# Cross attention's inverse sums: from a TensorE turn to a round trip through DRAM

## The reference, cut to what matters

```python
x = x + attn(layernorm(x), ...)
x = x + xattn(layernorm(x), ctx, ctx, mask, ...)     # the change is here
x = x + ffn(layernorm(x), ...)

# xattn, per sample b and head h (hc = 32, s = 512)
scores  = q @ k.T / sqrt(hc) + relative_term          # (s, s)
weights = softmax(scores, axis=-1)
context = weights @ v + relative_weights @ emb_v      # (s, hc)
out     = wo @ context                                # (256, s)
```

## Time and profile before

| what | us |
|---|---|
| median of 3 runs | 2598.54 |
| the profiled execution | 2598.18 |
| span of its instructions | 2596.4 |
| PE busy | 2411.5 |
| DVE busy | 2037.2 |
| ACT busy | 1128.8 |
| POOL busy | 1080.3 |
| distance of successive `near_back` (726.05 to 975.35, three rounds) | 83.1 |

### The profile page before, as it was taken

How to read it: one execution, slowest core, us unless ns; L and a number is a source line. 1 busy time by engine, 2 the same in 40 slices (tenths; PEclk the granted TensorE clock), 3 DMA queues, 4 the chain that set the end, 5 groups by cost and what they waited for, 6 DMA issues and landing times. The chain is left out here.

```text
span 2596.4 us, 40787 instructions
## 1 busy us (share of the span) xinstructions
PE 2411.5 (93%) x12856; PEld 1333.4 (51%) x12856; DVE 2037.2 (78%) x5965; ACT 1128.8 (43%) x2617; POOL 1080.3 (42%) x1564
## 2 busy tenths in 40 slices
PE   6889999999999999999988799999999999999985
PEld 4456655656566656665645344444444444444432
DVE  0466766777676776777664489999999999999997
ACT  1256666666666666666666221222222222222221
POOL 1133333333333333333332345555555555555552
PEclk9999999999999999999989899999999999999998
DMA  3034545444544545454446599999999999999996
GB/s 110 15 115 128 163 145 143 128 144 143 150 135 134 160 134 151 119 145 148 148 139 198 208 370 379 383 382 384 384 387 389 390 385 381 385 383 383 385 375 260
DMA packets 292741, 622.47 MB, mean 240 GB/s; under 512 B 162352, under 2 KB 163376, under 8 KB 292528
## 3 DMA queue, kind: packets, MB, share of 16 engines
q0 software_dynamic: 83968, 438.34, 44.4%
q1 hardware_dynamic: 174768, 80.85, 11.6%
q10 hardware_dynamic: 33792, 100.67, 11.3%
HBM read 577.80 MB, written 142.61 MB: 277 GB/s over the span
## 5 line engine op out<-in xcount | busy, mean ns | idle before, releaser
L1186 DVE CUSTOM_DVE_ANT_0 scores<-s_bank,added 128x512 f32<-128x512 f32 x512 | 350.2, 687 | 230.3 <-PE s_bank L661 185.4
L1501 PE MATMUL l_bank<-fold,xn_tf 128*128 128x512 f32 x992 | 435.5, 592 | 0.0
L996 ACT ACTIVATE probs<-scores,nmx 128x512 f32<-128x512 f32 x512 | 373.2, 729 | 129.4 <-DVE nmx L1186 125.4
L1479 POOL DMA_INDIRECT out_rows<-rows_out,rows_now x256 | 271.4, 1060 | 355.3 <-PE out_ps L1547 286.7
L1002 ACT COPY prob_t<-t_bank 128x512 f32<-128x512 f32 x512 | 299.3, 585 | 226.6 <-PE t_bank L671 226.1
L593 POOL TENSOR_TENSOR added<-mask_add,band 128x136 f32<-128x136 f32 (+1 forms) x512 | 247.6, 485 | 337.4 <-DVE nmx L1186 336.5
L1470 POOL DMA_INDIRECT in_rows<-rows_in,rows_now x256 | 310.3, 1212 | 134.3 <-DVE hid L1740 66.8
L639 PE MATMUL a_bank<-fold 128*128 128x256 f32 (+1 forms) x1024 | 305.2, 442 | 20.7 <-ACT fold L917 7.0
L671 PEld LDWEIGHTS t_bank<-ident,probs 128*128 128x128 f32 x2048 | 235.9, 141 | 165.5 <-issue 107.7
L671 PE MATMUL t_bank<-ident,probs 128*128 128x128 f32 x2048 | 313.4, 279 | 5.3 <-ACT prob_t L1002 3.2
L1593 ACT COPY sims<-l_bank 128x512 f32<-128x512 f32 x124 | 72.7, 586 | 555.5 <-PE l_bank L1501 555.5
(11 more groups left out here) (193 smaller groups left out, 3509.9 us busy)
## 6 DMA issues: line engine op xcount, KB each, us to landing
rows_in<-in_in_b_dram ACTq DMA_DIRECT2D x16, 2048.0 KB, 8.7
rows_out<-in_out_a_dram ACTq DMA_DIRECT2D x16, 2048.0 KB, 9.0
rows_in<-in_in_a_dram ACTq DMA_DIRECT2D x16, 1024.0 KB, 8.1
rows_out<-in_out_b_dram ACTq DMA_DIRECT2D x16, 1024.0 KB, 5.2
rel_scratch<-rel_pad SPq DMA_DIRECT2D x16, 640.0 KB, 3.0
band<-rel_scratch SPq DMA_DIRECT2D x512, 20.0 KB, 2.3
prob_scratch<-probs SPq DMA_DIRECT2D x512, 20.0 KB, 2.6
near<-prob_scratch SPq DMA_DIRECT2D x64, 156.1 KB, 3.1
```

Of the source, the lines that this page charges most:

```text
L996: nc.scalar.activation(prob_tile(s % PSLOTS), scores[:, s % 2, :], ACT.Exp, bias=nmx[:, s:s + 1], scale=-1.0, accum_out=lsum[:, s:s + 1]). ...
L1186: nc.vector.tensor_tensor_reduce(out=scores[:, s % 2, :], in0=s_bank[s % HPT][:, 0:L], in1=added[:, s % 2, :], scale=-1.0, scalar=-NEG, op ...
L1479: nc.gpsimd.indirect_dma_start(out_rows[:, h, :], None, rows_out, bass.IndirectOffsetOnAxis(rows_now[:, odd, h:h + 1], 0)).then_inc(out_lo ...
L1501: ins = nc.tensor.matmul(l_bank[c % 2][:], xn_t[:, k, :], fold[:, k, c * BANK:(c + 1) * BANK], start=(k == 0), stop=(k == KD - 1))
```

## The change

The widening copy (L1198), the wait before it, the turn on PE (L677) and the copy on ACT (L1007) are gone, with the step `SPREAD_LAG`. SP gets two new steps in each group. `store_sums` waits for `linv_ready`, now raised by the reciprocal, and writes the 128x4 inverse sums to DRAM turned, as 512 single elements. `spread_sums` waits until they have landed, and reads each of the four rows back to 32 partitions of `linv_t`, which now has two halves. `evict` waits for these four loads. `weigh` now waits only for `acc` to be emptied. Both steps stand after `store_windows` in SP's group; `near_back` moves between the two of group 7. The store of x3 and all that follows in the queue come behind them.

```diff
--- before.py
+++ after.py
@@ -139,7 +139,7 @@
         PACK, PB, OUT, X2, STATS3, POWER3, X3 = 4, 5, (6, 8), (7, 9), (10, 11), 12, 16
         LOAD_FOLD, FOLD, STORE_FOLD = 8, 29, 4
         EARLY_TURN, EARLY_SIMS, EARLY_SEARCH, EARLY_PICK = 11, (14, 18, 22, 26), (2, 2, 3, 3), 6
-    TURN_LAG, SUM_LAG, SPREAD_LAG, WEIGH_LAG, EVICT_LAG = 3, 5, 6, 8, 9
+    TURN_LAG, SUM_LAG, WEIGH_LAG, EVICT_LAG = 3, 5, 8, 9
     TOP_STEPS = 2 * TOPK // 8
     FOLD_VALUES_AT = 16
     SCORE_LATE = (16, 20)
@@ -223,6 +223,7 @@
         return FOLD_JOBS.index((kind, n))
 
     rel_scratch = nc.dram_tensor("rel_scratch", [(P + 1) * ROW], F32, kind="Internal").ap()
+    linv_dram = nc.dram_tensor("linv_dram", [2, HPT, P], F32, kind="Internal").ap()
     prob_scratch = nc.dram_tensor("prob_scratch", [(P + 1) * ROW], F32, kind="Internal").ap()
 
     with ExitStack() as ctx:
@@ -299,8 +300,7 @@
         nmx = sb("nmx", [P, STEPS])
         lsum = sb("lsum", [P, STEPS])
         linv = sb("linv", [P, STEPS])
-        linv_wide = sb("linv_wide", [P, HPT, HC])
-        linv_t = sb("linv_t", [P, P])
+        linv_t = sb("linv_t", [P, 2, P])
         probs = sb("probs", [P, PSLOTS * PROW])
         prob_t = sb("prob_t", [P, 2, HPT, QT_N, P])
         raw_q, raw_k = (prob_t[:, i].rearrange("p g k q -> p (g k q)").rearrange("p (k d) -> p k d", d=D)
@@ -356,8 +356,8 @@
         added_ready = sem("added_ready")
         exp_done = sem("exp_done")
         linv_ready = sem("linv_ready")
-        linv_turned = sem("linv_turned")
-        linv_kept = sem("linv_kept")
+        linv_stored = sem("linv_stored")
+        linv_loaded = [sem(f"linv_loaded{i}") for i in range(2)]
         near_written = [sem(f"near_written{i}") for i in range(2)]
         near_loaded = sem("near_loaded")
         near_packed = sem("near_packed")
@@ -448,6 +448,22 @@
                     n = ROW - QUAD + 1
                     sp.dma_start(near[g * QUAD:(g + 1) * QUAD, :, :].rearrange("r s w -> r (s w)")[:, 0:n],
                                  src[:, 0:n]).then_inc(near_loaded, 16)
+
+            def store_sums(r, n):
+
+                wait(sp, linv_loaded[n % 2], (r * (GROUPS // 2) + n // 2) * 16 * HPT)
+                sp.wait_ge(linv_ready, r * GROUPS + n + 1)
+                with nc.allow_non_contiguous_dma(reason="512 single elements"):
+                    sp.dma_start(linv_dram[n % 2].rearrange("h q -> q h"),
+                                 linv[:, n * HPT:(n + 1) * HPT]).then_inc(linv_stored, 16)
+
+            def spread_sums(r, n):
+
+                sp.wait_ge(linv_stored, 16 * (r * GROUPS + n + 1))
+                wait(sp, acc_emptied, r * GROUPS + n - 1)
+                for g in range(HPT):
+                    sp.dma_start(linv_t[g * HC:(g + 1) * HC, n % 2, :],
+                                 linv_dram[n % 2, g].partition_broadcast(HC)).then_inc(linv_loaded[n % 2], 16)
 
             def write_relative(b):
 
@@ -494,10 +510,12 @@
                         load_band(n + 2 - GROUPS)
                     if cross_in_round(b):
                         store_windows(r, n)
+                        store_sums(r, n)
+                        if n == GROUPS - 1:
+                            near_back(r)
+                        spread_sums(r, n)
                     if n == 4 and tail_in_round(b):
                         store(x3_dram, x3, x3_ready, x3_stored, b - 2, CT)
-                if cross_in_round(b):
-                    near_back(r)
 
             rounds(round_)
             sp.wait_ge(x3_stored, B * 16)
@@ -671,15 +689,10 @@
                     ins = nc.tensor.transpose(bank[:, k * P:(k + 1) * P], src[:, k * P:(k + 1) * P], ident[:])
                 ins.then_inc(t_filled, 1)
 
-            def spread(r, n):
+            def weigh(b, s, r, n, values):
+
+                o = n // QT_N
                 wait(pe, acc_emptied, r * GROUPS + n)
-                pe.wait_ge(linv_ready, r * GROUPS + n + 1)
-                nc.tensor.transpose(acc, linv_wide[:].rearrange("p g c -> p (g c)"), ident[:]).then_inc(linv_turned, 1)
-
-            def weigh(b, s, r, n, values):
-
-                o = n // QT_N
-                pe.wait_ge(linv_kept, r * GROUPS + n + 1)
                 pe.wait_ge(t_emptied, t_job(*((b, "PT", s - 2) if s >= 2 else (b - 1, "PT", s - 2 + STEPS)))[1] + 1)
                 for k in range(QT_N):
                     for g in range(HPT):
@@ -874,8 +887,6 @@
                         turn(b, s, *turn_at(b, s))
                     if s in SCORE_LATE and cross_in_round(b):
                         score(b - 1, s, p)
-                    if group_at(b, s, SPREAD_LAG):
-                        spread(*group_at(b, s, SPREAD_LAG))
                     if tail_in_round(b):
                         finish(b, s)
                     if group_at(b, s, WEIGH_LAG):
@@ -1002,10 +1013,6 @@
                 nc.scalar.copy(prob_t[:, n // HPT % 2, n % HPT, :, :].rearrange("p k q -> p (k q)"),
                                bank[:]).then_inc(t_emptied, 1)
 
-            def keep_spread(r, n):
-                act.wait_ge(linv_turned, r * GROUPS + n + 1)
-                nc.scalar.copy(linv_t[:], acc).then_inc(linv_kept, 1)
-
             def f_full(kind, n=0):
                 act.wait_ge(f_filled, f_job(kind, n) + 1)
                 return s_bank[f_job(kind, n) % HPT]
@@ -1055,8 +1062,6 @@
                                 lay_rows(b - 1, src, dst)
                     if turn_at(b, s):
                         turned(b, s, *turn_at(b, s))
-                    if group_at(b, s, SPREAD_LAG):
-                        keep_spread(*group_at(b, s, SPREAD_LAG))
                     if cross_in_round(b):
                         exponentials(b - 1, s)
                     if tail_in_round(b):
@@ -1192,16 +1197,16 @@
                 dve.wait_ge(exp_done, r * STEPS + (n + 1) * HPT)
                 if n == 0:
                     wait(dve, near_packed, r)
+                wait(dve, linv_stored, 16 * ((r - 1) * GROUPS + n + 1))
                 some = slice(n * HPT, (n + 1) * HPT)
-                nc.vector.reciprocal(linv[:, some], lsum[:, some])
-                self_wait(dve)
-                nc.vector.tensor_copy(linv_wide[:], linv[:, some].unsqueeze(2).to_broadcast([P, HPT, HC])).then_inc(
-                    linv_ready, 1)
+                nc.vector.reciprocal(linv[:, some], lsum[:, some]).then_inc(linv_ready, 1)
 
             def evict(r, n):
                 o, t = divmod(n, QT_N)
                 dve.wait_ge(acc_done, r * GROUPS + n + 1)
-                nc.vector.tensor_tensor(cn_t[:, o, t * P:(t + 1) * P], acc, linv_t[:], ALU.mult).then_inc(acc_emptied, 1)
+                dve.wait_ge(linv_loaded[n % 2], (r * (GROUPS // 2) + n // 2 + 1) * 16 * HPT)
+                nc.vector.tensor_tensor(cn_t[:, o, t * P:(t + 1) * P], acc, linv_t[:, n % 2, :],
+                                        ALU.mult).then_inc(acc_emptied, 1)
 
             def finish(b, s, p):
 
```

More of the change, by code:

```diff
@@ L672, in turn @@
                 ins.then_inc(t_filled, 1)
-            def spread(r, n):
-                wait(pe, acc_emptied, r * GROUPS + n)
-                pe.wait_ge(linv_ready, r * GROUPS + n + 1)
-                nc.tensor.transpose(acc, linv_wide[:].rearrange("p g c -> p (g c)"), ident[:]).then_inc(linv_turned, 1)
             def weigh(b, s, r, n, values):
                 o = n // QT_N
-                pe.wait_ge(linv_kept, r * GROUPS + n + 1)
+                wait(pe, acc_emptied, r * GROUPS + n)
                 pe.wait_ge(t_emptied, t_job(*((b, "PT", s - 2) if s >= 2 else (b - 1, "PT", s - 2 + STEPS)))[1] + 1)
```

## The result

| | before | after |
|---|---|---|
| median of 5 runs, us | 2598.54 | 3593.56 |
| span of the profiled execution | 2596.4 | 3591.7 |
| `near_back` to `near_back`, middle of the pass | 83.1 | 143.8 |
| `near_back` of the first and the last sample | 230.3, 1450.7 | 286.8, 2443.6 |
| PE's clock in a middle round | 1.00 | 0.80 |

The ratio of the runs is 1.3817, 95% interval 1.3797 to 1.3837. The forecast was 2590.5, the range ended at 2640. Fifteen distances between successive `near_back` are 143.8 us on average ((2443.63 - 286.78) / 15). Of the 995 us by which the span grew, 56 are lost before the first `near_back`, 936 between the first and the last, and 2 behind it. Before, the same fifteen distances are 81.4 us on average and not 83.1, because the last two are only 75.3 and 68.9; PE works 64.1 and 57.6 us in these, and 79.1 in the one before them.

What follows compares the result with a forecast made beforehand. PE was taken to bound the first pass, busy 78.2 of 82.6 us a round. From 2598.18 us, -13 (PE) -5 (DVE) +0 (steady rounds) +10 (last round) gave 2590.2, as median 2590.5; range 2577 to 2640, 8 in 10.

Steps and rivals of the forecast that it cites:

- the price of the store: SP's wait for 512 single elements to land: 2.6 us undisturbed, 6.8 beside an ACT table copy.
- slow store: Rival: the single-element store takes 5 us rather than 2.6, overrunning SP's chain and delaying evictions: about 2650 us, chance 0.08.
- the steady rounds' added waits: Waits added by SP's order in steady rounds: 0, bounds 0 and 5 us per round, earlier gaps absorbing delays.
- The overrun rival: SP's queue overruns, `near_back` slips into ACT's copy: 2.5 us per round plus 10, 2647 us (half: 2627); chance 0.3.
- SP's chain: SP's steps from group 5's inverse to group 7's sums: 18.6 us undisturbed, leaving 1.9 us to spare before `near_back` slips.
- the decision: Whether SP's order holds at `near_back`: issued from 728.7 instead of 726.05, landed 733.2, 1.8 us before DVE's pack.
- the last round: Last round with cross attention: a later band load for POOL and 2 us for `near_back`, 10 us, bounds 0 and 18.
- 80 us of SP's row: In the overrun rival, SP's issues and waits over one round added up to 80 of 83.1 us.
- The removals: Instructions gone from PE, DVE and ACT: 13, 5 and 0 us, together 18, bounds 0 and 50.
- DVE's 5 us: Gain from dropping DVE's widening copy and drain where PE waits for DVE: a third of at most 14.7 us.
- four steps of fixed length: From inverse to eviction, 10.4 us on average, against a trip of 5.6 us undisturbed, 13.2 beside a copy.
- The signs named for it: In the trace after: DVE idle before `evict`, DMA-released, once a round; late `near_back`; POOL's last-round band wait above 5.46 us.

Runs made afterwards that it cites:

- own_line: The kernel after with the 512 stored elements 64 bytes apart in DRAM and the loads reading a weight instead of the stored sums: 2694.4 us.
- gone_only: The kernel before with only the removals (widening copy, turn on PE, ACT copy), no round trip, eviction multiplying by a constant: 2581.2 us, ratio 0.9932.
- invert_first: The kernel after with DVE's invert of a group put ahead of the eviction of the group before it in the same step: 3452.4 us.

## Why the prediction was wrong

**The step that failed** is the price of the store: "I take 2.6 us, and 6.8 beside a copy (bounds 5.1 and 8.1)", and for the store alone an upper bound of 2.9 us. Measured, from the issue to the first load, was never less than 8.23, in the median 9.99. The bounds were made from stores of 128 runs of 160 bytes and a count of packets. That count was right, in the wrong place: 512 single elements 64 bytes apart land after 1.77 us, as quick as 128 of them. What no row could show is what it costs that these 512 are neighbours in DRAM. The range was called a bound from both sides, but its upper end held only for operations like those in the trace.

A rule had been put against it: the Trainium skill ("DMA: Bandwidth & Descriptors", Rules for kernel authors) gives 19 times for a transpose by access pattern, an estimate of 49 us for a store. That overstated the store by a factor of five, and the runs show that the transposed pattern alone isn't slow (own_line has it too, at 1.77 us); yet by it the forecast would have had the right sign. Eight waits of 9.4 us are 75 us per round, nearly the whole period of before. The rival "slow store", 2650 with a chance of 0.08, was the case that came, and its own 5 us were too low as well. With no row for single elements, its chance should have been far larger.

**The second step that failed**, shown by own_line: "I take 0 for the steady rounds' added waits". With a store at the price that I had forecast (median 2.41 us, 3.95 at the third quartile) the time is 2694, not 2590. A round is then 87.4 us ((1546.48 - 235.05) / 15). The overrun rival had the place, SP's chain, but 49 us for 96, and it put the cost into `near_back`. The chain was added up at undisturbed values only, along one stretch of the round; in own_line POOL waits for bands 33.4 us and DVE at the eviction 36.6 us from 700 to 1200 us, ten times each in six rounds. `near_back`, on which I had set the decision, cost 4.2 us there and hardly mattered.

The distances say more than their mean. Against gone_only the first thirteen are 5.3 us longer each, just over the bound of 5, and the last two 15.5 and 24.3 us (87.2 and 90.0 instead of 71.7 and 65.7). The prediction gave the last round 10 us, at most 18, and looked for them in one late band load. It had itself counted 80 us of SP's row in a round of 83.1, but it took all rounds for 83.1 us, though the last two were 75.3 and 68.9 in the kernel before. SP's row is as long there as elsewhere (143.2 and 151.9 us in the kernel after), so these two alone lose 40 of the 108 us between the first and the last `near_back`.

**The removals** were right in sum: 18 forecast, 18 measured. In place they were not: 1.2 us per round was forecast and in the middle 0.7 came, while the last two distances gave 6.9 together. DVE's 5 us were not found, so that the parts made up the right sum is luck.

**The loads** cost 9 us (2590.1 against 2581.2), two thirds of it in the last two distances; the forecast had none in the middle rounds and 10 in the last, but for loads and stores together. That 2590.1 equals the forecast is therefore chance.

**What follows from a slow store** wasn't worked out either. The rival "slow store" added the longer trip to the chain of two stores only. With eight waits of 9.4 us SP's whole row is longer than a round and becomes the round: 134.6 us even with the loop open (invert_first). The loop came on top, at most 9.2 us a round: the prediction compared the trip with four steps of fixed length and has no sentence on what happens past that length, when the eviction that waits stands before the next inverse on the same engine. The signs named for it did show, above all DVE idle before `evict`, but in 125 of 128 groups instead of once a round.

**Right** were: PE as the bound of a middle round before, the instructions that go, that SP would stand in front of bands and `near_back`, and POOL's longer wait for bands.

## What to carry to other kernels

Where a change adds a transfer of a shape that the trace doesn't hold, bound it by count, by size and by where the pieces lie, and leave the upper end open if one of the three has no row. Don't write single elements side by side into DRAM: spread them, or write runs of 16 bytes and let the reader take the stride. When a wait comes into an in-order queue, add up the queue's whole row for one period, issues and waits; where the sum is longer than the period, it is the new period, and in rounds that are shorter than the others it is reached first. Then ask whether what stands behind the wait feeds the same wait again, for such a loop can be longer than the row.

## What the runs showed of the hardware

- 512 single 4-byte elements stored to DRAM side by side took at least 8.2 us from the issue to the next step of the queue that waited for them, 64 bytes apart 1.8 us; the issue took 0.38 us in both.
- The DMA engines' last packet of either store started 1.3 us after the issue in the median; the extra 6.5 us lay between it and the landing; where no other transfer ran, the engines had no packet in that stretch.
- A fourth of the elements at the same density took 6.5 us; in another order 6.0. Two side by side and the next 64 bytes off cost nothing extra.
- Such a store slows DMAs that nobody makes wait for it: a 2 MB DRAM to DRAM copy landed after 18.2 instead of 9.0 us (9.5 with the spread store), and the kernel before became 1.15 times as long by the dense store alone.
- PE's granted clock was 0.80 over a round in which it was idle for a third of the time, against 1.00 in a round in which it was busy for 95%, and its busy time for nearly the same work was a fifth longer.
